# Normalising and the first tap moved to ScalarE, and an order of its own for the first turn of layer 1

## Chip, cores and metric

One core of one Trainium2 chip. The metric is the device time of one execution in microseconds; of three runs of the kernel before, the median was 862.69 us (862.49 to 867.14). Instructions run on five engines, each with a queue of its own that is worked through in order: TensorE (PE), VectorE (DVE), ScalarE (ACT), GpSimd (POOL) and SyncE (SP, which issues the DMAs). They meet at semaphores only.

## The reference

Two layers over x of shape (8, 256, 256), that is 2048 rows of 256. Each layer computes `x = x + attn(layernorm(x)) + ffn(layernorm(x))`.

Layer 0: softmax attention over 8 key heads with 4 query groups, plus a memory term, and a gated FFN of 2048 columns with 4-bit weights. Layer 1, which the change is about:

```python
xc = silu(causal_conv(xn, conv_w, taps=4) + conv_b)          # depthwise, along the sequence
q, k = l2n(xn @ Wq.T), l2n(xn @ Wk.T)                        # 16 heads of 16
v = ln(xn @ Wv.T) * vn_g + vn_b
i = sigmoid(xc @ ig_w.T + ig_b); gamma = sigmoid(xc @ gamma_w.T + gamma_b)
mem[t] = gamma[t] * mem[t-1] + i[t] * k[t] * v[t]            # scan along the sequence
o = ln(ln(mem) * q) * gn_g + gn_b
attn = (o * sigmoid(xc @ og_w.T + og_b)) @ Wo.T
ffn = (sigmoid(xn @ T1.T) * (xn @ T2.T)) @ T3.T              # T: weights rounded to -1, 0, 1; 704 columns
```

## The kernel before

Every factor of a matrix product is split into a high part (rounded to the format that TensorE reads) and a low part, the remainder, so that a product is three products (high by high, high by low, low by high). The high part is made by ScalarE, the low part by VectorE or GpSimd (`xn_low`, `hidden_low`, `next_low`, `output_low`).

**Layer 0** (`layer0`, to 610.7 us of the trace) is a pipeline over 64 units, one head of one batch element and one FFN pair each; `schedule()` puts extra steps at units. In units 58 to 65 it also prepares layer 1: SyncE loads the raw weights, ScalarE rounds them (`next_high`, two halves a unit, from unit 60), GpSimd subtracts (`next_low(n)`, one a unit, units 61 to 64). SyncE then loads three pieces of the FFN's signs into the buffers that these leave; piece 2 needs `next_low(3)`. ScalarE copies the three pieces (`next_signs`), and each copy waits until all three have landed. After each batch element's FFN VectorE adds it to X and takes mean and variance for layer 1's norm, and GpSimd makes `rstd` of the variance (step `"mlp"`); for the last element GpSimd does so at the start of layer 1.

**Layer 1** (`layer1`) treats the rows in 4 groups of 512 (two batch elements b = 0, 1; 4 row tiles t; 2 column blocks k or m). The first half of a group's work (projections, convolution, gates, FFN up) is "early", the second half (scan, norms, output, FFN down) is "late". `turns` runs five turns `turn(late, early, ahead)`: (None, 0, 1), (0, 1, 2), (1, 2, 3), (2, 3, None), (3, None, None). "Ahead" is the start of the group behind the early one: normalise, transposes, first projections, first taps. I call them turn 0 to 4; turn 0 has no late group. What an engine does in a turn is written out by hand as a sequence of calls (`if late is not None: ...`), and this sequence is its queue.

The steps that the change touches:
- `normalise(g)`: four instructions, one a row tile of 256, `(x - mean) * rstd` into `xn`, on VectorE (L1445); TensorE transposes `xn` (`xn_turn`, L1668), ScalarE evicts it twice (`xn_high`, L1266 and L1267: `xn_hi` and the padded `xpad`).
- `convolve(g, taps)`: tap 0 is a `tensor_scalar` per column block (`x*w0 + bias`, L1457), taps 1 to 3 are `scalar_tensor_tensor` (L1460), all on VectorE. Then `convolved`: two sigmoids on ScalarE (L1306), the products on GpSimd (L1216), high part on ScalarE (L1310), low part on GpSimd (L1219).
- `query_key(g, t)`, `value(b)`, `gamma(m)`, `gate(t)` and `ffn_up(c)` on TensorE (L1649, L1702). `projected` (L1277, L1278), `values_squared`, `sigmoid(c)` (L1293), `hidden_high(c)` (L1300), `decays`, `gate` on ScalarE evict them.
- `norms()` on VectorE: sums of squares (L1472), an inverse root by steps (L1422 to L1429), the scaled values (L1482). `hidden(c)` on VectorE (L1489) is the FFN's product; chunk c + 1 on TensorE waits for `hidden(c)`.
- `values(b)` (four steps, L1118), `through_input_gate(b)` (L1152) and the late group's `memory_scaled`, `gated` (L1118): one half on VectorE, the other on GpSimd.

In turn 0 TensorE's sequence was: transposes, queries/keys 0 and 1, FFN chunk 0, 1, queries/keys 2, values 0, 1, chunk 2, queries/keys 3, chunk 3, gamma 0, chunk 4, gates 0, 1, chunk 5, group 1's transposes 0, gamma 1, gates 2, 3, transposes 1, group 1's queries/keys 0, 1. Then turn 1 begins with `b_turn` (L1755), which needs both halves of `through_input_gate`, and FFN chunk 0, which needs both halves of group 1's `xn_low`.

## Time and profile before

| what | us |
|---|---|
| median of 3 runs (lowest, highest) | 862.69 (862.49, 867.14) |
| profiled execution, its own time | 865.88 |
| its span | 864.0 |
| mean granted clock of TensorE | 0.938 |
| VectorE `L1445` normalise, 8 of them from 640 us on | 8.9 |
| ScalarE idle in front of `L1293`, 640 to 864 us | 40.6 |
| GpSimd `L1118` rows<-rows,par, 24 of them | 34.2 |

The span is the profiled execution from its first to its last instruction; its own time is 1.9 us more. Busy time of an engine says how full it is, not whether it sets the end. For that one looks at the timeline, where each row has the idle time of its engine before it and, behind the arrow, what ended it: the engine that is never idle in a stretch, or the waits handed from engine to engine, set its length. A granted clock of 1.0 is TensorE's level of 2.4 GHz, 0.5 that of 1.2 GHz; a figure between them is a mean over a stretch.

### The profile page before, as it was taken

Reading aid. Unit: us, or ns where it says so; the run is one execution under the profiler, and the core shown is the slowest. Engines: PE = TensorE matmul, PEld = TensorE weight load, DVE = VectorE, ACT = ScalarE, POOL = GpSimd, SP = SyncE. Lnnn points to the kernel's source line nnn. Section 1 sums busy time; section 2 is a strip of 40 time slices with the busy share of each in tenths; the row PEclk is TensorE's granted clock in tenths of the full one; section 3 lists DMA queues with packets and bytes.
Section 4 is the critical chain, followed back from the end, with each engine's and each line's share of the span. In section 5 each row is a group of like instructions: output and inputs, shape, how many; then the busy total and the mean of one; then the engine's idle time right before and its main releaser. Section 6 shows DMA issues by size and latency. Waiting matters only on the chain. (4 is left out here: it accounts for less than half of the span.)

```text
span 864.0 us, 15139 instructions
## 1 busy us (share of the span) xinstructions
PE 750.2 (87%) x5602; PEld 645.5 (75%) x5602; DVE 653.9 (76%) x1123; ACT 454.8 (53%) x722; POOL 420.1 (49%) x353
## 2 busy tenths in 40 slices
PE   3368799999999999999999999999568897888773
PEld 2266688888888888888888888887456686777672
DVE  6989877887777677686777777673664899998965
ACT  4246645655655655664665565565544453454411
POOL 2344444354257575667344435346354283663821
PEclk9579999999999999999999999999788899999985
DMA  5011121111001011011000000301100000000000
GB/s 156 25 38 39 38 76 44 48 36 45 20 15 38 24 47 46 20 50 27 9 21 10 12 21 3 93 3 41 48 0 1 0 1 25 1 17 10 0 25 24
DMA packets 22108, 25.88 MB, mean 30 GB/s; under 512 B 4499, under 2 KB 17171, under 8 KB 22037
## 3 DMA queue, kind: packets, MB, share of 16 engines
q1 hardware_dynamic: 22036, 24.93, 10.5%
q8 instruction: 45, 0.74, 0.3%
q14 instruction: 27, 0.21, 0.1%
HBM read 14.83 MB, written 3.28 MB: 21 GB/s over the span
## 5 line engine op out<-in xcount | busy, mean ns | idle before, releaser
L647 DVE TENSOR_REDUCE neg_max<-s_pair 128x4 f32<-128x1024 f32 x127 | 155.1, 1221 | 75.3 <-PE s_pair L861 75.1
L469 ACT ACTIVATE probs<-t_pair 128x1024 f32<-128x1024 f32 x128 | 131.2, 1025 | 136.8 <-PE t_pair L886 136.5
L366 POOL TENSOR_TENSOR hid<-g,hid 128x512 f32<-128x512 f32 x64 | 82.2, 1285 | 179.2 <-DVE g L758 146.1
L360 POOL TENSOR_TENSOR hid_lo<-hid,hid_hi 128x512 fp32r<-128x512 f32 x64 | 86.0, 1344 | 86.8 <-ACT hid_hi L492 86.7
L861 PE MATMUL s_pair<-K,Q 96*128 96x256 f32 x508 | 85.0, 291 | 15.6 <-DVE neg_max L647 9.2
L861 PEld LDWEIGHTS s_pair<-K,Q 96*128 96x128 f32 x508 | 75.8, 194 | 24.2 <-issue 8.1
L886 PE MATMUL t_pair<-Q,K 104*128 104x512 f32 x256 | 85.9, 417 | 0.3 <-DMA Q<-max_parts 0.3
L928 PE MATMUL down<-hi,hid_hi 128*128 128x256 f32 x256 | 84.0, 328 | 1.9 <-POOL hid_lo L360 1.9
L901 PE MATMUL misc<-probs,V 128*32 128x256 f32 x1024 | 69.2, 388 | 3.4 <-DVE kc L603 2.6
L928 PE MATMUL down<-lo,hid_hi 128*128 128x256 f32 x256 | 71.9, 281 | 0.0
L928 PE MATMUL down<-hi,hid_lo 128*128 128x256 f32 x256 | 71.7, 280 | 0.0
L1118 POOL TENSOR_TENSOR rows<-rows,par 128x512 f32<-128x512 f32 x24 | 34.2, 1425 | 71.6 <-DVE rows L1524 54.0
L928 PEld LDWEIGHTS down<-hi,hid_hi 128*128 128x128 f32 x256 | 48.1, 188 | 27.9 <-issue 24.9
L1702 PE MATMUL lbank<-lo,hi 128*128 128x512 f32 x192 | 54.7, 431 | 12.6 <-DVE l_hid L1489 12.3
L789 PE MATMUL gate<-xn_hi,hi 128*128 128x256 f32 x256 | 57.0, 304 | 0.0
L1702 PEld LDWEIGHTS lbank<-lo,hi 128*128 128x128 f32 x192 | 37.9, 205 | 25.0 <-DVE l_hid L1489 16.6
L750 DVE SCALAR_TENSOR_TENSOR g<-g,gate 128x512 f32<-128x512 f32 x64 | 42.7, 668 | 18.0 <-ACT g L495 17.9
L503 ACT ACTIVATE g<-g 128x512 f32<-128x512 f32 x64 | 40.2, 628 | 29.9 <-DVE g L750 29.9
L1649 PE MATMUL lbank<-hi,lo 128*128 128x512 f32 (+1 forms) x192 | 53.3, 378 | 1.2 <-DVE lo L1129 1.2
L789 PE MATMUL up<-xn_hi,hi 128*128 128x256 f32 x256 | 52.2, 286 | 0.0
L789 PE MATMUL up<-xn_lo,hi 128*128 128x256 f32 x256 | 51.9, 285 | 0.0
L789 PE MATMUL up<-xn_hi,lo 128*128 128x256 f32 x256 | 51.9, 285 | 0.0
(254 smaller groups left out, 1979.5 us busy)
## 6 DMA issues: line engine op xcount, KB each, us to landing
stage<-in_ternary SPq DMA_DIRECT2D x18, 256.0 KB, 2.8
Q<-q_hi SPq DMA_DIRECT2D x64, 64.0 KB, 2.0
stage<-in_scales SPq DMA_DIRECT2D x8, 384.0 KB, 3.4
X<-in_x SPq DMA_DIRECT2D x8, 256.0 KB, 4.2
Q<-q_lo SPq DMA_DIRECT2D x32, 64.0 KB, 2.0
Q<-max_parts SPq DMA_DIRECT2D x128, 4.0 KB
out<-X SPq DMA_DIRECT2D x8, 256.0 KB, 2.1
signs<-w_stage SPq DMA_DIRECT2D x9, 128.0 KB, 1.8
```

The source lines that it names most:

```text
L360: pool.tensor_tensor(hid_lo[:, m % 2, :, :].rearrange("p a n -> p (a n)"), hid[:, m % 2, :], hid_hi[:, m % 2, :, :].rearrange("p a n -> p ...
L366: pool.tensor_tensor(hid[:, m % 2, :], g[:, m % 2, :], hid[:, m % 2, :], ALU.mult).then_inc(S["hid_done"], 1)
L469: act.activation(probs[:, u % 2, th, :], t_pair[:], ACT.Exp, scale=SCALE).then_inc(S["probs_done"], 1)
L647: dve.tensor_reduce(neg_max[:, u % 2, 4 * jp:4 * jp + 4], score_banks(u, jp)[:].rearrange("p (s n) -> p s n", n=SEQ), AX_X, ALU.max, negat ...
L750: dve.scalar_tensor_tensor(out=g[:, m % 2, :], in0=g[:, m % 2, :], scalar=1.0, in1=gate[:], op0=ALU.add, op1=ALU.mult).then_inc(S["u_done" ...
L789: mm = pe.matmul(out, lhs[a][k], rhs[b][k], start=(n == 0), stop=(n == 3 * KC - 1))
L861: mm = pe.matmul(score_banks(u, jp)[:, 512 * j + SEQ * s:512 * j + SEQ * s + SEQ], Q[0:KROWS, quad, 2 * jp + j, P * s:P * s + P], K[0:KROW ...
L886: mm = pe.matmul(t_pair[:, 512 * jp:512 * jp + 512].rearrange("p (j n) -> p j n", j=2), K[rows, quad, hq, P * th:P * th + P], Q[rows, quad ...
L901: mm = pe.matmul(misc[32 * j:32 * j + 32, 0:SEQ], V[:, th, h, :], probs[:, u % 2, th, SEQ * j:SEQ * j + SEQ], start=(th == 0), stop=(th == ...
L928: mm = pe.matmul(down[:, D * t:D * t + D], h[:, m % 2, n, P * t:P * t + P], w[:, a, n, 2 * D:3 * D], start=(a == 0 and t == 0 and n == 0 a ...
L1649: mm = pe.matmul(dst, lhs[a](k), rhs[b](k), start=(n == 0), stop=(last and n == 3 * KC - 1))
L1702: mm = pe.matmul(banks[bank][:], w[:, k, P * c:P * c + P], x[:, k, :], start=(n == 0), stop=(n == 3))
```

## The change

1. `normalise` moves from VectorE to ScalarE, in all turns: `Identity` with `scale=rstd` and `bias=shift`, both per row. `shift = -mean * rstd` is new: two GpSimd instructions of two columns behind each batch element's `rstd` in layer 0, and two at the start of layer 1. In turns 1 and 2 ScalarE does it between `convolved` and `output_squared(0)`.
2. Tap 0 moves to ScalarE as `first_tap` (semaphore `conv_first`), in turns 0, 1 and 2 ahead of the next group's `projected(0)`. `conv_step` counts 6 instead of 8.
3. `next_low` runs one unit earlier in layer 0.
4. Turn 0 gets sequences of its own on all engines. The other turns keep theirs, other than for 1 and 2. `norms` is cut in two (`norms_summed`, `norms`), one behind the other in the later turns; `convolved` on ScalarE likewise (`convolution_gated`).

```diff
-                    pool.tensor_tensor(rs, rs, half[:], ALU.pow)
+                    pool.tensor_tensor(rs, rs, half[:], ALU.pow).then_inc(S["pool_link"], 1)
+                    sh = keep["shift"][:, 2 * b:2 * b + 2]
+                    pool.wait_ge(S["pool_link"], linked())
+                    pool.tensor_tensor(sh, keep["mv"][:, 2 * b:2 * b + 2, 0], rs, ALU.mult).then_inc(S["pool_link"], 1)
+                    pool.wait_ge(S["pool_link"], linked())
+                    pool.tensor_scalar(sh, sh, -1.0, None, ALU.mult)
...
-                if 0 <= u - NEXT_AT - 3 < 4:
-                    next_low(u - NEXT_AT - 3)
+                if 0 <= u - NEXT_AT - 2 < 4:
+                    next_low(u - NEXT_AT - 2)
...
+                def normalise(g):                      # on ScalarE
+                    ...
+                    for t in range(TPG):
+                        one = slice(g * TPG + t, g * TPG + t + 1)
+                        x = flat(X[:, one, :]).rearrange("p (j k) -> p k j", k=KC)
+                        inc(act.activation(xn[:, t, :, :], x, ACT.Identity, scale=rstd[:, one], bias=shift[:, one]), "xn_ready")
+                def first_tap(g):
+                    ...
+                        inc(act.activation(dst, xpad[:, k, :, 0:SEQ], ACT.Identity, scale=conv[:, k, 0:1], bias=conv[:, k, TAPS:TAPS + 1]), "conv_first")
...
                 if late is None:                       # GpSimd, turn 0
                     xn_low(pool, early, 1)
                     scaled()
+                    convolved()
+                    output_weights()
+                    hidden_low(pool, early, 1)
+                    values(pool, early, 0)
+                    hidden_low(pool, early, 2)
+                    through_input_gate(pool, early, 0)
+                    hidden_low(pool, early, 3)
+                    through_input_gate(pool, early, 1)
+                    hidden_low(pool, early, 4)
+                    hidden_low(pool, early, 5)
+                    xn_low(pool, ahead, 1)
+                    return
...
                 if late is None:                       # ScalarE, turn 0
+                    normalise(early)
                     xn_high(early, 0)
                     xn_high(early, 1)
-                    constants()
+                    act.wait_ge(once["loaded"], 16 * N_LOADS)
+                    first_tap(early)
+                    gate_constants()
                     projected(early, 0)
                     projected(early, 1)
+                    values_squared(0)
+                    values_squared(1)
+                    projected(early, 2)
+                    projected(early, 3)
+                    convolution_gated()
+                    sigmoid(0)
+                    output_weights()
+                    convolved()
+                    hidden_high(0)
+                    hidden(1)
+                    gate(0)
+                    hidden(2)
+                    normalise(ahead)
+                    decays(0)
+                    gate(1)
+                    hidden(3)
+                    gate(2)
+                    gate(3)
+                    hidden(4)
+                    decays(1)
+                    hidden(5)
+                    xn_high(ahead, 0)
+                    xn_high(ahead, 1)
+                    queries_kept()
+                    hidden_high(5)
+                    first_tap(ahead)
+                    projected(ahead, 0)
+                    projected(ahead, 1)
+                    return
...
                 if late is None:                       # VectorE, turn 0
-                    normalise(early)
                     xn_low(dve, early, 0)
-                    convolve(early, range(0, 2))
+                    convolve(early, range(1, TAPS))
                     ...                                # the gates' bias
+                    norms_summed()
+                    hidden(0)
+                    norms()
+                    hidden(1)
+                    hidden_low(dve, early, 0)
+                    values(dve, early, 1)
+                    for c in range(2, FFN_CHUNKS):
+                        hidden(c)
+                    xn_low(dve, ahead, 0)
+                    convolve(ahead, range(1, 2))
+                    return
...
                     query_key(early, 1)                # TensorE, turn 0
+                    value(0)
+                    value(1)
+                    query_key(early, 2)
+                    query_key(early, 3)
+                    ffn_up(0)
+                    ffn_up(1)
+                    gate(0)
+                    ffn_up(2)
+                    gamma(0)
+                    gate(1)
+                    ffn_up(3)
+                    gate(2)
+                    gate(3)
+                    ffn_up(4)
+                    gamma(1)
+                    ffn_up(5)
+                    xn_turn(ahead, 0)
+                    xn_turn(ahead, 1)
+                    query_key(ahead, 0)
+                    query_key(ahead, 1)
+                    return
```

## Rows read from the trace of the kernel before

**Rows 1.** The page's engine table: busy us (share of the span) xinstructions.

```profile
PE 750.2 (87%) x5602; PEld 645.5 (75%) x5602; DVE 653.9 (76%) x1123; ACT 454.8 (53%) x722; POOL 420.1 (49%) x353
```

**Rows 2.** Busy by stretch: us; PE, PEld, DVE, ACT, POOL busy; granted clock; DMA, GB/s.

```profile
611.00:662.90 51.90, 40.33 (x168) 32.15 (x168) 31.20 (x47) 27.04 (x48) 23.79 (x26) 0.84 0.06 14
662.90:721.70 58.80, 48.46 (x249) 40.29 (x249) 52.25 (x87) 26.05 (x47) 33.19 (x25) 0.91 0.00 1
...
612.50:621.00 8.50, 7.30 (x21) 5.80 (x22) 6.21 (x9) 4.59 (x9) 5.13 (x6) 0.51 0.30 81
...
643.00:649.00 6.00, 5.83 (x16) 4.62 (x17) 5.04 (x7) 1.36 (x3) 5.76 (x6) 0.57 0.00 0
...
729.00:734.00 5.00, 5.00 (x18) 4.03 (x17) 4.76 (x12) 1.10 (x3) 1.77 (x2) 0.66 0.00 0
```

**Rows 3.** Timeline, end of layer 0, GpSimd, ScalarE, VectorE: start, us, what [idle before].

```profile
595.32 1.85 POOL L354 TENSOR_TENSOR lo<-queries,hi 128x768 fp32r<-128x768 f32 x1
...
601.43 1.84 POOL L354 TENSOR_TENSOR lo<-w_stage,hi 128x768 fp32r<-128x768 f32 x1
603.23 1.72 POOL L360 TENSOR_TENSOR hid_lo<-hid,hid_hi 128x512 fp32r<-128x512 f32 x1
610.92 0.53 POOL L1190 MEMSET rows<- 128x512 f32 x1 [5.98 <-POOLq L109]
...
606.42 2.86 ACT L482 ACTIVATE hi<-stage 128x1536 fp32r<-128x1536 bf16 x2 [4.05 <-DMA w_stage<-signs]
...
608.19 0.25 DVE L629 BATCH_NORM_AGGREGATE l_mv<-stats 128x2 f32<-128x6 f32 x2
```

**Rows 4.** Timeline of GpSimd, a batch's end in layer 0.

```profile
566.85 0.20 POOL L347 TENSOR_SCALAR l_rstd<-l_mv 128x2 f32<-128x2 f32 x1
...
569.33 1.29 POOL L360 TENSOR_TENSOR hid_lo<-hid,hid_hi 128x512 fp32r<-128x512 f32 x1 [1.51 <-ACT hid_hi L492]
```

**Rows 5.** Timeline, layer 1, turns 0 and 1: TensorE and GpSimd.

```profile
624.86 2.11 PE L1702 MATMUL lbank<-lo,hi 128*128 128x512 f32 x8 [1.97 <-DVE l_hid L1489]
...
643.17 2.05 PE L1649 MATMUL lbank<-lo,hi 128*128 128x512 f32 x4 [6.61 <-POOL lo L1219]
...
666.74 3.75 PE L1702 MATMUL lbank<-lo,hi 128*128 128x512 f32 x8 [0.22 <-POOL lo L1129]
...
664.09 1.25 POOL L1152 TENSOR_TENSOR rows<-qk,gates 128x512 f32<-128x512 f32 x1
```

**Rows 6.** Timeline of ScalarE around the start of layer 1.

```profile
599.88 0.38 ACT L513 ACTIVATE o_sb<-misc 128x256 f32<-128x256 f32 x1
...
616.25 0.71 ACT L1251 ACTIVATE o_hi<-rows,const 128x512 fp32r<-128x512 f32 x1
616.86 0.61 ACT L1252 ACTIVATE lo<-rows 128x512 fp32r<-128x512 f32 x1
```

**Rows 7.** Timeline of VectorE, layer 1.

```profile
624.72 1.38 DVE L1445 TENSOR_SCALAR rows<-X,l_mv,l_rstd 128x256 f32<-128x256 f32 x4
...
634.31 3.41 DVE L1472 TENSOR_REDUCE ss<-sq 128x96 f32<-128x1536 f32 x2
...
643.54 0.68 DVE L1489 TENSOR_TENSOR l_hid<-sig,lbank 128x512 f32<-128x512 f32 x1
...
672.84 0.69 DVE L1513 TENSOR_REDUCE sm<-osq 128x32 f32<-128x512 f32 x1 [2.40 <-ACT osq L1343]
...
678.41 4.46 DVE L1445 TENSOR_SCALAR rows<-X,l_mv,l_rstd 128x256 f32<-128x256 f32 x4
...
713.97 2.86 DVE L1457 TENSOR_SCALAR shared<-xpad,conv 128x512 f32<-128x512 f32 x2
...
740.94 0.68 DVE L1489 TENSOR_TENSOR l_hid<-sig,lbank 128x512 f32<-128x512 f32 x1
```

**Rows 8.** Timeline, end of turn 1: GpSimd's gating, VectorE's low parts.

```profile
710.73 3.06 POOL L1118 TENSOR_TENSOR rows<-rows,par 128x512 f32<-128x512 f32 x2 [2.96 <-DVE rows L1558]
...
716.75 1.28 DVE L1563 TENSOR_TENSOR o_lo<-lbank,o_hi 128x512 fp32r<-128x512 f32 x2
```

More of the change, by code:

```diff
@@ L1199, in _ @@
             pool.tensor_tensor(rstd[:, last], rstd[:, last], half[:], ALU.pow).then_inc(once["rstd_done"], 1)
+            pool.wait_ge(once["rstd_done"], 2)
+            pool.tensor_tensor(shift[:, last], mv[:, last, 0], rstd[:, last], ALU.mult).then_inc(once["rstd_done"], 1)
+            pool.wait_ge(once["rstd_done"], 3)
+            pool.tensor_scalar(shift[:, last], shift[:, last], -1.0, None, ALU.mult).then_inc(once["rstd_done"], 1)
             def scaled():
@@ L1233, in turn @@
                     through_input_gate(pool, early, 0)
-                if late is not None:
-                    gated(pool, late, 0)
+                gated(pool, late, 0)
                 if early is not None:
@@ L1374, in turn @@
                     hidden(3)
+                    convolution_gated()
                     convolved()
-                if late is not None:
-                    output_squared(0)
+                if ahead is not None:
+                    normalise(ahead)
+                output_squared(0)
                 if early is not None:
@@ L1381, in turn @@
                     sigmoid(4)
-                if late is not None:
-                    output_squared(1)
+                output_squared(1)
                 if early is not None:
@@ L1398, in turn @@
                     hidden_high(5)
-                if late is not None:
-                    for b in halves:
-                        output_high(b)
+                for b in halves:
+                    output_high(b)
                 if ahead is not None:
+                    first_tap(ahead)
                     projected(ahead, 0)
@@ L1683, in value @@
                     wait("xpad_done", b + 1)
+                    wait(f"xn_lo_done{b}", 1)
                     wait("decay_done", 0)
@@ L1804, in turn @@
                     ffn_up(3)
-                if late is not None:
-                    ffn_down(0)
-                    ffn_down(1)
+                ffn_down(0)
+                ffn_down(1)
                 if early is not None:
@@ L1823, in turn @@
                     query_key(ahead, 1)
-                if late is not None:
-                    for b in halves:
-                        o_turn(b)
-                    for b in halves:
-                        output(b)
+                for b in halves:
+                    o_turn(b)
+                for b in halves:
+                    output(b)
             turns(turn)
```

128 lines of the change are left out of this document (57 added, 71 removed).

## The prediction

> **What bounds the kernel now.** I read the engine table first [rows 1]: TensorE is busy 87% of the span, VectorE 76%, ScalarE 53%, GpSimd 49%. That average mixes two stages, so I went on to the stretches [rows 2]. Layer 0 ends at 610.7; layer 1 is five turns from 611 to 864. In turn 0 (611 to 662.9) VectorE works 31.2 of 51.9 us and TensorE 40.3: neither is full, so waits set it. In turn 1 (662.9 to 721.7) VectorE works 52.25 of 58.8: there VectorE is the bound, and turn 2 is alike. The timeline of turn 1 confirms it: VectorE has two gaps, of 2.4 us each, near the start (the second in [rows 7]), and hardly any from 673.7 on. The last two turns issue what they did before, so I take them as unchanged.
>
> In what follows all times are on the trace's own clock; "new" times of turn 0 leave the earlier start of layer 1 out and it is added at the end.
>
> **Part A, the weight splits one unit earlier.** GpSimd's last `next_low` runs at 601.43 for 1.84 us, ahead of the last `hidden_low`, which runs from 603.23 to 604.95; the last down product waits for that, and VectorE's last aggregate, behind the product, ends at 608.44 [rows 3]. SyncE issues the third load of signs only when that `next_low` is done, at 603.3; it lands 3.1 us later. ScalarE waits 4.05 us for it, starts the three sign copies at 606.42 and ends them at about 610.7 (1.43 each). Layer 1's first GpSimd instruction is at 610.92. One unit earlier the fourth `next_low` stands at 595.32, where the third is now, done at 597.17; the load is issued then and lands some 3.1 us later, 600.3. ScalarE copies from 602.3 on, three times 1.43: done at 606.6. `hidden_low` starts when its input is there, 602.4, ends about 603.7, the product starts 1.25 us earlier, VectorE ends at 608.44 - 1.25 = 607.2. That is now the later one: layer 1 starts at about 607.5, 3.4 us earlier. Least: 1.5 (a copy is late for another reason); most: 3.6, ScalarE's path. The first `next_low` has to wait for a copy that ScalarE makes earlier in its queue than anything GpSimd needs next, and falls into an idle time like that before `hidden_low` at 569.33: nothing.
> GpSimd's two new tiny operations (the shift) follow each batch's power, seven times: 0.2 us each and a gap (the scale at 566.85 took 0.20). Behind them GpSimd idles 1.51 us before `hidden_low` at 569.33 [rows 4]: hidden; if not, 0.6 us times 7.
>
> **Part B, turn 0.** Today the chain runs through GpSimd: TensorE waits 6.61 us at 643.17 for the low part of the convolution, since ScalarE comes to the convolution's sigmoids only behind four FFN chunks; at the turn's end the second input gate runs from 664.09 to 665.34 on GpSimd and TensorE's transposes and chunk 0 of turn 1 (666.74) come after it [rows 5]. The new order, step by step:
> Normalise on ScalarE. The trace has no 256-wide instruction there with two pointer operands. A plain one takes 0.38 us (599.88); of two 512-wide ones the one with a pointer scale takes 0.71 (616.25), the other 0.61 (616.86) [rows 6]: 0.38 + 0.1 + 0.1 = 0.58, less 0.1 of overlap as between those two, about 0.48 each, 1.9 for four against VectorE's 1.38 [rows 7]. Bounds 0.3 and 0.7 each. TensorE's eight transposes, at half clock, take about as long and cover it: the first two tiles are ready at 612.65 instead of 612.4, and the evictions start at 613.7, as before. The first tap is 0.61 + 0.2 - 0.1 = 0.7 each, 616.05 to 617.5, and the first projection is ready only at 618.6; VectorE's taps 1 to 3, six of them, end by 622.3 at 0.9 each, and nobody asks for them before 628.9. The Trainium skill, "ScalarE: Activation LUTs", on the ACTIVATE instruction, gives 186 ns + 0.833 ns an element and 93 ns more for each pointer operand. By it four rows are 2.0 us and two taps 1.4; the trace agrees on the pointer operand (0.10 us in rows 6), and the rule speaks against moving them only where ScalarE is late.
> TensorE: queries/keys 0 and 1 end at 620.9, as now, at a granted clock of 0.51, the 1.2 GHz level [rows 2]. From there a 512-wide pass is 0.23 us (eight in 2.11 with the tail [rows 5]): values 2.9 (24 passes of half the width), to 623.8; queries/keys 2 and 3, 1.4 each, to 626.6; FFN chunk 0 (1.85) to 628.4. ScalarE squares the last projection by 627.7, loads its table (1.28) to 628.9, does the convolution's two sigmoids (1.1) to 630.0 and chunk 0's to 630.6. VectorE's two square sums end at 629.5, `hidden(0)` at 631.2, the norms at 637.0 (today the sums take 3.41 from 634.31 on and the norms end at 643.54, so 5.8 [rows 7]), `hidden(1)` at 637.7. GpSimd meanwhile has the convolution's four operations (5.3 us today, at 1.3 each), from 629.6 to 634.8. So TensorE idles from 628.4 to 631.3, does chunk 1, waits to 634.8, does gate 0 and starts chunk 2 at 637.8, behind the norms. Here I expect the clock to be halved for some us, as it was after the idle time before 643 (0.57) [rows 2]; up to 637.8 that costs nothing, since the norms end last.
> From 637.8: chunk 2, gamma 0, gate 1 (1.85 + 1.4 + 1.6) to 642.7; chunk 3 waits for `hidden(2)`, behind `values(1)` on VectorE (2.8 beside an idle GpSimd, 4.0 beside a busy one), 643.1; chunk 3, gates 2 and 3, chunk 4, gamma 1 to 651.4; chunk 5 to 653.3; transposes to 654.0. Then ScalarE's evictions to 655.0, VectorE's low part to 655.8, queries/keys of group 1 to 658.6, the two input transposes to 659.6. ScalarE: queries kept by 657.1, `hidden_high(5)` 657.7, GpSimd `hidden_low(5)` 659.0 and `xn_low` 660.3. So chunk 0 of turn 1 starts at 660.3 where it was 666.74 [rows 5]; the scans, behind one tap on VectorE, end at 662.4 where they ended at 667.8.
> At 666.74 the clock was low, chunk 0 took 3.75 where eight passes take 2.11 at full clock, the centring as much longer, and VectorE waited 2.40 us at 672.84 [rows 5, 7]; at turn 2's start neither was so. I expect turn 2's picture: centring from 662.2 to 664.1, squares to 664.7, VectorE's sums from 665.1 to 666.4 where they end at 674.43 (the second 0.9 behind the row of 672.84): 8.0 us earlier. Were the clock low there, 5.3; were it full throughout and layer 1 begun warm, 10.5.
>
> **Part C, normalise and first tap in turns 1 and 2.** The four normalising instructions take VectorE 4.46 us in turn 1 and 4.45 in turn 2, but 1.38 in turn 0: in the former GpSimd works beside them. The two first taps take 2.86 beside GpSimd [rows 7], and 1.0 without it. Both leave VectorE. How much of it arrives? In turn 2: the norm ends at 731.99; `hidden(1)` has its sigmoid at 731.9 and runs at once; the scaling, low part and centring take 4.0, to 736.6. Then `hidden(2)` needs chunk 2, and TensorE, at a clock of 0.66 from 729 to 734 [rows 2], comes to it only at 736.4: product to 738.3, sigmoid to 738.9, `hidden(2)` at 738.9 against 740.94 [rows 7]. So 2.0 of the 4.45 arrive; at full clock 3.6 would; 0.5 if TensorE or the sigmoid slips as much again. ScalarE's own 1.9 us go in ahead of `output_squared(0)` at 748.32, behind which it idles 2.6 us: nothing. The same holds for turn 1.
> Of the first tap 0.25 arrives: with it gone VectorE is ready at 714.0, but it then needs `o_hi`, which hangs on GpSimd's gating (from 710.73, 3.06 and 1.3 us, to 715.14), TensorE's transposes and an eviction, together to 716.5; its two low parts begin at 716.75 today [rows 8]. ScalarE does the taps after `o_hi`, 716.9 to 718.4, just before VectorE wants them at 717.7. Bounds: 0 and, GpSimd being freed of contention, 1.0. Together 2.25 a turn, 4.5 for two.
>
> **Sum.** 3.4 + 8.0 + 4.5 = 15.9 us. The profiled execution took 865.88 for a span of 864.0; it becomes 850.0. The median of the runs shown, 862.69, is 3.2 lower; from it 846.8, which I predict.
>
> **Rivals.**
> One, the clock stays up: TensorE, with fewer gaps, is at full clock when layer 1 starts (the pause before it shrinks from 5.9 to about 4 us) and at the middle of turns 1 and 2. Then B is 10.5 and C 2 x 3.9: 841. For it: turn 0 ran at full clock from 621 to 636 with a pause of 2.0 in it. Against: at 729 to 734 it was 0.66 behind a pause of 2.7 which stays. Chance 0.18.
> One more on that side: VectorE stays the bound to the end of turns 1 and 2, and all of what it is relieved of arrives, 4.45 + 2.86 a turn, 14.6 for two: 3.4 + 8.0 + 14.6 = 26.0, 836.7. For it: 52.25 busy of 58.8 [rows 2]. Against: TensorE comes to chunk 2 only at 736.4, and `o_hi` only at 716.5. Chance 0.03. The Trainium skill, "GPSIMD Engine Reference", section Specifications, says that the SBUF interfaces are shared with VectorE, with contention for instructions in a two-port mode or with two SBUF inputs. The 4.46 against 1.38 us [rows 7] agree, and by it VectorE's other instructions with two SBUF inputs would keep their own contention.
> Two, less arrives: VectorE's gain in turns 1 and 2 is met by TensorE at half clock (0.5 each), and turn 0's handover stays at the low clock (5.3): 3.4 + 5.3 + 1.0 = 9.7, 853. Chance 0.2.
> Three, layer 0's end doesn't move, as another wait holds the copies, and two holds as well: 856.4; with turn 0's chain longer by 3 us, 859. Chance 0.06 for all of the near-nothing cases (over 858.4).
> Four, slower: the norms stand between `hidden(0)` and `hidden(1)` on VectorE, so TensorE has gaps from 628.4 to 637.8 and could stay at 1.2 GHz for the rest of turn 0. What lies behind 637.8 is 18.4 us of passes (four chunks at 1.85, two gammas, three gates, transposes, two queries/keys); doubled, chunk 0 of turn 1 starts at 680 instead of 666.74, 13.5 later, and with A and C off it is +5.6: 868. It decides from about 14 us of extra passes on. Against: after the pause of 6.6 the clock, 0.57 from 643 to 649 [rows 2], was full again after that. Chance 0.03.
>
> **Chances and range.** The forecast (844 to 850.5 as its own range) has 0.50. A measurement of this kernel tells 0.5%, 4.3 us, from no change. Faster 0.91, same 0.06, slower 0.03. The range leaves out the 836.7, the first rival's far end, and cases three and four: 839 to 854.
>
> **What would show it.** A: the gap before ScalarE's sign copies gone, GpSimd's first memset of layer 1 at 607.5. B: TensorE's longest wait in turn 0 under 3 us, chunk 2 behind the norms, turn 1's scans ending at 659 on the new clock. C: no wait for `hidden(1)`, one of about 1 us or less before `hidden(2)`, one of 2.5 us before the low parts of o. Wrong would be: more than 3 us of waiting ahead of `hidden(2)`, a projection late behind ScalarE's normalise, or turn 0 longer than 49 us.

## The result, and the profile after

The changed kernel takes 850.32 us (median of 4 runs, 848.63 to 851.37), the kernel before, run beside it, 863.62 (862.49 to 867.14). The medians are 13.3 us apart. The ratio over all executions, which is not exactly that of the medians, is 0.9833, with a 95% interval of 0.9806 to 0.9861: 14.4 us faster (12.0 to 16.8). All gains below are worked out from such ratios, each against executions of the kernel before that ran beside it. The profiled execution took 849.49 us for a span of 847.5, 16.5 less than the 864.0 of before, at a mean granted clock of 0.949 (0.938).

The engine table of the page, to be read beside [rows 1]: VectorE gives up 20 us of busy time, ScalarE takes on 14. TensorE is busy 8 us less for the same number of matmuls, since fewer of them ran at the lower clock.

```profile
PE 742.0 (88%) x5602; PEld 638.1 (75%) x5602; DVE 633.5 (75%) x1099; ACT 468.4 (55%) x746; POOL 423.2 (50%) x369
```

The stretches that answer to [rows 2]. The first three lines are turns 0, 1 and 2, here cut at VectorE's first sums of the memory's centred squares (`sm<-osq`) in turns 1 to 3 ([rows 2] cuts earlier, where the scans start, so its lines and these don't compare one to one); the other lines are where the granted clock fell, or didn't.

```profile
607.60:663.60 56.00, 44.17 (x196) 35.03 (x196) 30.84 (x43) 36.70 (x65) 27.86 (x30) 0.88 0.05 13
663.60:716.00 52.40, 46.20 (x248) 39.27 (x248) 45.49 (x81) 27.87 (x50) 29.40 (x22) 0.93 0.03 11
716.00:765.80 49.80, 43.44 (x248) 36.73 (x248) 45.30 (x81) 28.32 (x51) 29.88 (x22) 1.00 0.03 11
...
628.00:636.00 8.00, 5.72 (x17) 4.03 (x18) 7.69 (x14) 3.40 (x7) 4.98 (x4) 0.80 0.00 0
...
664.00:672.00 8.00, 6.44 (x28) 5.47 (x29) 6.82 (x18) 2.36 (x5) 2.79 (x3) 0.79 0.00 0
705.00:711.00 6.00, 5.04 (x28) 4.83 (x28) 4.61 (x6) 3.83 (x7) 2.26 (x2) 0.72 0.13 44
717.00:723.00 6.00, 5.00 (x29) 4.43 (x30) 5.66 (x16) 2.38 (x5) 1.42 (x2) 1.00 0.00 0
```

Those sums make good milestones: every kernel has them and little overlaps across them. The distances from one to the next, read from the profiled execution of every kernel of this study (us; "start" is GpSimd's first memset of layer 1, and all kernels but the first two are described below):

| kernel | span | start | turn 0 | turn 1 | turn 2 | turn 3 | rest |
|---|---|---|---|---|---|---|---|
| before | 864.0 | 610.92 | 61.92 | 53.88 | 54.55 | 51.48 | 31.25 |
| after | 847.5 | 607.63 | 56.01 | 52.43 | 49.77 | 50.86 | 30.80 |
| e1_split_early | 858.6 | 608.35 | 60.28 | 55.10 | 54.87 | 49.26 | 30.74 |
| e2_moves | 858.4 | 611.23 | 62.54 | 51.66 | 51.34 | 50.84 | 30.79 |
| e3_order_only | 857.4 | 610.65 | 54.70 | 54.84 | 54.51 | 51.46 | 31.24 |
| e4_norm_alone | 858.2 | 611.54 | 61.90 | 52.03 | 52.65 | 49.31 | 30.77 |
| e5_norm_only | 857.7 | 610.94 | 62.01 | 52.02 | 52.65 | 49.31 | 30.77 |
| e6_tap_only | 864.3 | 610.13 | 63.21 | 53.50 | 54.76 | 51.49 | 31.21 |
| e7_fill | 844.3 | 607.43 | 56.35 | 50.23 | 50.37 | 48.86 | 31.06 |
| e8_high_first | 845.5 | 605.82 | 54.89 | 51.36 | 51.38 | 51.01 | 31.04 |
| e9_no_moves | 845.9 | 605.78 | 54.59 | 52.04 | 51.73 | 50.96 | 30.80 |
| e10_twice | 847.0 | 606.02 | 56.47 | 51.36 | 51.38 | 50.93 | 30.84 |
| e11_both | 840.6 | 606.98 | 55.30 | 49.22 | 49.22 | 48.88 | 31.00 |
| e12_both_no_moves | 847.1 | 606.92 | 55.61 | 50.88 | 52.97 | 49.45 | 31.27 |

So the 16.5 us of the span came from: start 3.29, turn 0 5.91, turn 1 1.45, turn 2 4.78, turns 3 and 4 1.07. The table also shows how far to trust one execution: e1 runs the same layer 1 as before, and its single turns differ by 0.3 to 2.2 us, with a TensorE that was at the lower clock in other places. What a part is worth is therefore taken from the ratios, and the profile is used for where it happens.

**The end of layer 0**, GpSimd and then ScalarE, beside [rows 3]. The fourth `next_low` is gone from between 601.43 and 603.23; `hidden_low` starts when its input is there, the sign copies follow without a wait.

```profile
595.17 1.86 POOL L359 TENSOR_TENSOR lo<-w_stage,hi 128x768 fp32r<-128x768 f32 x1
...
600.03 1.29 POOL L371 TENSOR_TENSOR hid<-g,hid 128x512 f32<-128x512 f32 x1 [1.75 <-DVE g L763]
602.28 1.27 POOL L365 TENSOR_TENSOR hid_lo<-hid,hid_hi 128x512 fp32r<-128x512 f32 x1 [0.96 <-ACT hid_hi L497]
607.63 0.52 POOL L1195 MEMSET rows<- 128x512 f32 x1 [4.08 <-POOLq L109]
...
602.11 2.85 ACT L487 ACTIVATE hi<-stage 128x1536 fp32r<-128x1536 bf16 x2
604.86 1.47 ACT L487 ACTIVATE hi<-w_stage 128x1536 fp32r<-128x1536 bf16 x1
608.24 2.14 ACT L1288 ACTIVATE rows<-X,l_shift,l_rstd 128x256 f32<-128x256 f32 x4 [1.92 <-POOL half L1197]
```

**The middle of turn 0**, VectorE and TensorE, beside [rows 5, 7]: `hidden(0)`, the norms (their first and last instruction), `hidden(1)`; then FFN chunks 1 and 2. The wait of 6.61 us for the convolution's low part is gone; in its place stand 3.03 and 1.82, both for VectorE. The clock was low behind the first: chunk 1 takes 3.42, chunk 2 2.14.

```profile
627.58 0.69 DVE L1556 TENSOR_TENSOR l_hid<-sig,lbank 128x512 f32<-128x512 f32 x1 [1.19 <-ACT sig L1335]
628.18 1.16 DVE L1541 SCALAR_TENSOR_TENSOR ss<-ss,eps 128x192 f32<-128x192 f32 x1
...
634.82 0.68 DVE L1556 TENSOR_TENSOR l_hid<-sig,lbank 128x512 f32<-128x512 f32 x1
...
628.32 3.42 PE L1765 MATMUL lbank<-lo,hi 128*128 128x512 f32 x8 [3.03 <-DVE l_hid L1556]
...
635.55 2.14 PE L1765 MATMUL lbank<-lo,hi 128*128 128x512 f32 x8 [1.82 <-DVE l_hid L1556]
```

**The handover to turn 1**: ScalarE, VectorE, GpSimd, TensorE. ScalarE has its queue without a gap from 651.6 on; its first taps come last before VectorE's tap 1, which waits 2.70 us for them and then runs beside GpSimd's `xn_low`.

```profile
653.50 1.09 ACT L1370 ACTIVATE q_kept<-qk 128x1024 f32<-128x1024 f32 x1
654.45 0.29 ACT L1371 ACTIVATE rq<-ss 128x64 f32<-128x64 f32 x1
654.59 0.66 ACT L1342 ACTIVATE hi<-l_hid 128x512 fp32r<-128x512 f32 x1
655.11 1.54 ACT L1296 ACTIVATE shared<-xpad,conv 128x512 f32<-128x512 f32 x2
...
656.10 2.66 DVE L1525 SCALAR_TENSOR_TENSOR shared<-xpad,conv,shared 128x512 f32<-128x512 f32 x2 [2.70 <-ACT shared L1296]
658.68 2.41 DVE L1572 TENSOR_TENSOR_SCAN rows<-shared,lbank 128x256 f32<-128x256 f32 x4
661.01 2.71 DVE L1525 SCALAR_TENSOR_TENSOR shared<-xpad,conv,shared 128x512 f32<-128x512 f32 x4
663.64 1.27 DVE L1580 TENSOR_REDUCE sm<-osq 128x32 f32<-128x512 f32 x2
...
655.33 1.29 POOL L1140 TENSOR_TENSOR lo<-l_hid,hi 128x512 fp32r<-128x512 f32 x1 [3.83 <-ACT hi L1342]
656.58 1.63 POOL L1134 TENSOR_TENSOR lo<-xpad,lo 128x512 fp32r<-128x512 f32 x1
...
658.47 2.06 PE L1765 MATMUL lbank<-lo,hi 128*128 128x512 f32 x8 [1.08 <-POOL lo L1134]
660.36 1.95 PE L1826 MATMUL lbank<-const,rows 128*128 128x128 f32 x16
```

**Turns 1 and 2**, VectorE and TensorE, beside [rows 7, 8]: `hidden(1)`, `hidden(2)`, the first sum of squares, the low parts of o. Chunk 1 on TensorE waits for `hidden(0)`, 3.25 us in turn 1 and 2.41 in turn 2; behind the longer wait the clock was low (3.55 against 2.12 us).

```profile
669.78 0.69 DVE L1556 TENSOR_TENSOR l_hid<-sig,lbank 128x512 f32<-128x512 f32 x1 [0.80 <-ACT sig L1335]
...
675.87 0.69 DVE L1556 TENSOR_TENSOR l_hid<-sig,lbank 128x512 f32<-128x512 f32 x1 [0.88 <-ACT sig L1335]
676.48 3.40 DVE L1536 TENSOR_REDUCE ss<-sq 128x96 f32<-128x1536 f32 x2
...
705.03 1.29 DVE L1630 TENSOR_TENSOR o_lo<-lbank,o_hi 128x512 fp32r<-128x512 f32 x2 [2.46 <-ACT o_hi L1398]
...
721.34 0.68 DVE L1556 TENSOR_TENSOR l_hid<-sig,lbank 128x512 f32<-128x512 f32 x1
...
726.85 0.69 DVE L1556 TENSOR_TENSOR l_hid<-sig,lbank 128x512 f32<-128x512 f32 x1 [0.42 <-ACT sig L1335]
...
665.56 3.55 PE L1765 MATMUL lbank<-lo,hi 128*128 128x512 f32 x8 [3.25 <-DVE l_hid L1556]
...
718.00 2.12 PE L1765 MATMUL lbank<-lo,hi 128*128 128x512 f32 x8 [2.41 <-DVE l_hid L1556]
```

### The profile page after: what moved, and what is told of

It reads as the page before. It is cut to its first block and busy times, and to the rows that moved or that the text cites. A ratio compares the mean times of both kernels' runs of the same rounds, so it can differ in the third digit from the quotient of the medians.

```text
span 847.5 us, 15157 instructions
## 1 busy us (share of the span) xinstructions
PE 742.0 (88%) x5602; PEld 638.1 (75%) x5602; DVE 633.5 (75%) x1099; ACT 468.4 (55%) x746; POOL 423.2 (50%) x369
## 5 line engine op out<-in xcount | busy, mean ns | idle before, releaser
L1711 PE MATMUL lbank<-hi,lo 128*128 128x512 f32 (+1 forms) x192 | 51.0, 367 | 2.8 <-ACT lo L1308 1.6
```

The lines of the kernel that those rows point to most:

```text
L1711: mm = pe.matmul(dst, lhs[a](k), rhs[b](k), start=(n == 0), stop=(last and n == 3 * KC - 1))
```

## Experiments: the parts one by one

**e1_split_early: part A alone.**

```diff
-                if 0 <= u - NEXT_AT - 3 < 4:
-                    next_low(u - NEXT_AT - 3)
+                if 0 <= u - NEXT_AT - 2 < 4:
+                    next_low(u - NEXT_AT - 2)
```

> The kernel before with part A alone: next_low one unit earlier. Theory: layer 1's first GpSimd instruction moves from 610.9 to 607.6 and nothing else changes, so 3.3 us off (859.4 from 862.7), with all of layer 1 shifted as a block. Rival: the copies of the signs are not what layer 0's end waits for in the end, or the shorter pause changes TensorE's clock at the start of layer 1: then under 1 us or over 5 us.

861.93 us against 864.94, ratio 0.9978 (0.996 to 0.9995): 1.9 us, with an interval of 0.4 to 3.5; the medians are 3.0 apart. Within one execution the distance from GpSimd's last `hid<-g` to its first memset of layer 1 is cleaner, as it leaves out how long the rest of layer 0 took: 10.73 us before (600.19 to 610.92), 7.60 in the changed kernel, 7.32 here. Part A is worth 3.1 to 3.4 us at its place, and the ratio allows that only at the end of its interval. The two figures differ by the moves: from the last `hidden_low` to that memset it is 5.35 or 5.36 us in the five kernels that have both part A and the moves to ScalarE (after, e7, e8, e10, e11), and 5.07 in the three that have part A without the moves (e1, e9, e12).

**e3_order_only: turn 0's order alone**, with normalise and tap 0 on VectorE and `next_low` where it was. Against the changed kernel:

```diff
                 if late is None:                       # VectorE, turn 0
+                    normalise(early)
                     xn_low(dve, early, 0)
-                    convolve(early, range(1, TAPS))
+                    convolve(early, range(0, TAPS))
...
                     for c in range(2, FFN_CHUNKS):
                         hidden(c)
+                        if c == 2:
+                            normalise(ahead)
                     xn_low(dve, ahead, 0)
-                    convolve(ahead, range(1, 2))
+                    convolve(ahead, range(0, 2))
```

> The kernel before with turn 0's new sequences on all engines, but normalise and tap 0 still on VectorE (the next group's normalise behind hidden(2)) and the old place of next_low. Theory: the reordering by itself takes about 6 us off (5 in turn 0, the rest as TensorE starts turn 1 at full clock): 856 to 857.5. Rival: the order only pays because ScalarE took work off VectorE in turn 0, and here VectorE ends the turn late: under 2 us off.

859.52 us, ratio 0.9937 (0.9912 to 0.9963): 5.4 us. In the profile turn 0 is 7.2 us shorter, more than in the changed kernel (5.9), and turns 1 to 4 are within 1.0 us of before.

**e2_moves: normalise and tap 0 on ScalarE, in the old order of turn 0.** It has points 1 and 2 of the change, and none of 3 and 4.

> The kernel before with normalise and tap 0 on ScalarE, the old order in turn 0 and the old place of next_low. Theory: 2.0 to 3.4 us in each of turns 1 and 2 ahead of the sums of squares, 0.25 behind, nothing in turn 0: 4.5 to 7 us off, 856 to 858. Rival one: all that VectorE is relieved of arrives, 14 us off. Rival two: the moves pay only with the new turn 0, so under 1.5 us off here.

860.37 us, ratio 0.994 (0.9919 to 0.9962): 5.2 us. Turns 1 and 2 are 2.2 and 3.2 shorter, turn 0 is 0.6 longer. The three parts alone add up to 1.9 + 5.4 + 5.2 = 12.5 us of the 14.4, the same within their intervals (by the medians 3.0 + 5.4 + 4.6 = 13.0 of 13.3).

**e5_norm_only and e6_tap_only: the two moves apart.** e5 has `normalise` and `shift` of the change in the kernel before, e6 has `first_tap`.

> The kernel before with the normalisation alone moved to ScalarE (old order of turn 0, first taps stay on VectorE). Theory: normalise carries nearly all of the gain of turns 1 and 2 (together 5.4 us for both moves): turns 1 and 2 shorter by 2 to 3 us each, turn 0 level, since there VectorE doesn't bind, 860.0 us. Rival: the taps carry part, since with them off VectorE its low parts of o come earlier by more than 0.25 us: 861.5 us.

> The kernel before with the first tap alone moved to ScalarE. Theory: 0.25 us a turn at most, since VectorE's low parts of o then wait for o_hi instead (a wait of 2.4 to 2.6 us before them), and in turn 0 ScalarE comes to the taps no earlier than VectorE did, up to 0.6 us lost there: level with before within 0.1%, 864 against 864 us. Rival: the 2.86 us of two taps beside GpSimd arrive in turns 1 and 2: 3 to 5 us faster.

e5: 857.04 us, ratio 0.9919 (0.9888 to 0.9949), 7.0 us; by the profile turns 1 and 2 are 1.9 shorter each. e6: 865.44 us, ratio 1.0007 (0.9986 to 1.0028); turn 0 is 1.3 longer, turns 1 and 2 together 0.2 shorter. What the moves gained in the kernel before came from normalising, as far as the times can tell; part of the 7.0 may be turn 3, 2.2 shorter in e5's profile, though the change leaves that turn alone.

**e4_norm_alone: the same four instructions on VectorE, only earlier.** In the kernel before, VectorE's normalise stood behind `memory_normed`, where GpSimd is busy; here it stands ahead of it, where GpSimd is idle. Nothing leaves VectorE.

```diff
+                if ahead is not None:
+                    normalise(ahead)
                 if late is not None:
                     memory_normed()
-                if ahead is not None:
-                    normalise(ahead)
```

> The kernel before with one change: VectorE's normalise of the next group stands ahead of memory_normed, where GpSimd is idle, and not behind it, where GpSimd works. If contention with GpSimd makes the four instructions 4.46 us, they take about 1.4 here in turns 1 and 2, hidden(2) comes 2 us earlier in each and the kernel is 3 to 5 us faster (858 to 860). If their length belongs to them, they stay at 4.4 and the time stays within 1 us or gets longer.

859.94 us, ratio 0.994 (0.9917 to 0.9963): 5.2 us, as much as e2. VectorE in turn 1 (compare 4.46 in [rows 7]):

```profile
675.53 1.38 DVE L1445 TENSOR_SCALAR rows<-X,l_mv,l_rstd 128x256 f32<-128x256 f32 x4
...
686.11 0.69 DVE L1489 TENSOR_TENSOR l_hid<-sig,lbank 128x512 f32<-128x512 f32 x1 [0.74 <-ACT sig L1293]
686.72 3.41 DVE L1472 TENSOR_REDUCE ss<-sq 128x96 f32<-128x1536 f32 x2
```

Four instructions that cost 4.46 us beside GpSimd cost 1.38 without it. In turn 1 the sum of squares starts 13.28 us behind the first of `sm<-osq` here, the same 13.28 in e5 and 15.13 before: 1.85 arrive whether 3.1 us of VectorE's time go or all 4.46. The rest goes mostly to waits that then appear, for chunk 2's sigmoid (0.74 here, 1.02 in e5) and in e5 for chunk 1's too (0.75), and to instructions that now run beside GpSimd (in e5 `hidden_low(0)` takes 1.26 us, here 0.72).

**e9_no_moves: the changed kernel with both moves taken back** and e4's place for normalise. If moving work to ScalarE is what matters, this one loses it.

> Turn 0's new order and the early next_low, but normalise and tap 0 stay on VectorE, with normalise ahead of memory_normed in turns 1 and 2, where GpSimd is idle. Theory (contention, not the engine, made normalise dear; the three parts add up): layer 1 takes within 2 us of what it takes in the changed kernel, 848 to 852. Rival (the moves to ScalarE are worth their 5 to 7 us on top): 854 to 857.

850.23 us, ratio 0.9831 (0.9802 to 0.986): level with the changed kernel. Layer 1 took 240.12 us of the span, there 239.87. The balance has two sides: turn 0 is 1.4 us shorter than in the changed kernel, and turns 1 and 2 together are 1.0 longer than in e8 and e10, which have the moves. VectorE at the handover, to be read beside the changed kernel's:

```profile
651.85 1.00 DVE L1504 TENSOR_SCALAR shared<-xpad,conv 128x512 f32<-128x512 f32 x2 [0.29 <-ACT xpad L1282]
652.77 1.41 DVE L1507 SCALAR_TENSOR_TENSOR shared<-xpad,conv,shared 128x512 f32<-128x512 f32 x2
655.13 2.42 DVE L1555 TENSOR_TENSOR_SCAN rows<-shared,lbank 128x256 f32<-128x256 f32 x4 [0.95 <-PE lbank L1820]
657.47 2.71 DVE L1507 SCALAR_TENSOR_TENSOR shared<-xpad,conv,shared 128x512 f32<-128x512 f32 x4
660.37 0.69 DVE L1563 TENSOR_REDUCE sm<-osq 128x32 f32<-128x512 f32 x1 [0.18 <-ACT osq L1361]
```

VectorE did tap 0 in 1.0 us at 651.85, in time that it otherwise idles, tap 1 in 1.41 ahead of GpSimd's `xn_low`, and now waits for TensorE before the scans. With tap 0 on ScalarE, turn 0 is 56.01, 56.35 and 56.47 us (after, e7, e10), without it 54.70 and 54.59 (e3, e9): the move costs 1.6 us there. This is the price in this order of ScalarE's queue, not of the move as such. Where `hidden_high(5)` goes first (e8, e11 and e12, below), turn 0 is 54.89 and 55.30 with the move and 55.61 without it: VectorE's tap 1 then runs beside GpSimd's `hidden_low(5)` as well as its `xn_low`, and takes 3.38 us in e12.

```profile
654.27 3.38 DVE L1507 SCALAR_TENSOR_TENSOR shared<-xpad,conv,shared 128x512 f32<-128x512 f32 x2
```

**e10_twice: is ScalarE's work free in turns 1 and 2?** The changed kernel, writing the four normalised tiles twice in each of these turns.

```diff
                 if ahead is not None:
-                    normalise(ahead)
+                    normalise(ahead, True)             # the four instructions two times
```

> The changed kernel; in turns 1 and 2 ScalarE writes the four normalised tiles twice, 2.1 us more of its time in each. Theory: ScalarE has slack there and nothing gets longer, within 0.5 us a turn. Rival: ScalarE is so near the chain that the 2 us come back, at least in part, through hidden_high(3) and the evictions behind it: 1 to 2 us a turn.

848.69 us, ratio 0.9813 (0.979 to 0.9836). The second set (2.15 us at 684.41) is there in the trace. Turns 1 and 2 are 51.36 and 51.38 us, together 0.5 more than in the changed kernel (52.43 and 49.77) and the same as in e8 (51.36 and 51.38), which writes them once: no loss. ScalarE's side of the move is free, with at least 2.1 us of room.

## Experiments: what holds the changed kernel, and a faster one

**e7_fill.** In turns 1 to 3 TensorE waits for `hidden(0)` ahead of FFN chunk 1, and VectorE is then late for `hidden(2)`. Here queries/keys 2 and value 0, which need nothing of VectorE, go ahead of chunk 1, and ScalarE's evictions follow.

```diff
                     ffn_up(0)                          # TensorE
-                    ffn_up(1)
                     query_key(early, 2)
                     value(0)
+                    ffn_up(1)
...
-                    hidden_high(0)                     # ScalarE
-                    hidden(1)
                     projected(early, 2)
                     values_squared(0)
+                    hidden_high(0)
+                    hidden(1)
                     values_squared(1)
```

> The changed kernel; in turns 1 to 3 TensorE does queries/keys 2 and values 0 ahead of FFN chunk 1 (in the pause of 2.4 to 3.3 us in which it waits for hidden(0)), and ScalarE evicts them before hidden_high(0). If it is TensorE's pause and the low clock behind it that hold hidden(2) back, chunk 1 runs in about 2.1 us instead of 3.55 in turn 1, VectorE no longer waits for hidden(1) and hidden(2), and the sums of squares come 2.5 to 3 us earlier in turn 1, 0.4 in turn 2, 2 in turn 3: 3 to 6 us less than the changed kernel. If VectorE was the bound there all along, under 1 us.

843.69 us, ratio 0.9758 (0.9725 to 0.9791), against the changed kernel's 0.9833. TensorE in turn 1; VectorE has no wait before `hidden(1)` and `hidden(2)`:

```profile
665.69 2.11 PE L1765 MATMUL lbank<-lo,hi 128*128 128x512 f32 x8 [0.43 <-DVE l_hid L1556]
...
674.02 0.68 DVE L1556 TENSOR_TENSOR l_hid<-sig,lbank 128x512 f32<-128x512 f32 x1
674.62 3.40 DVE L1536 TENSOR_REDUCE ss<-sq 128x96 f32<-128x1536 f32 x2
```

The wait is 0.43 instead of 3.25 us, chunk 1 runs at full clock (2.11 us instead of 3.55), and turns 1 to 3 are 2.2, -0.6 and 2.0 shorter. Turn 2 had been at full clock in the changed kernel's profile; here the clock was low at its end (0.86 from 755 to 766), which costs 1.1 us. From the sums to the first sum of squares it is 10.84 us in both turns, against 12.84 and 11.39 in the changed kernel and 12.97 to 12.99 in e8 and e10.

That distance, and the two behind it, tell the parts apart better than whole turns. From the sums to the sum of squares, in turns 1 and 2: 15.13 and 14.82 before, 13.28 and 12.87 in e4, 13.28 and 12.88 in e5. From the sum of squares to the low parts of o: 28.77 to 28.82 in the seven kernels with the first tap on VectorE (before, e1, e3, e4, e5, e9, e12), 28.54 to 28.58 in the seven with it on ScalarE. From there to the next sums: 9.82 to 9.97 or 10.85 to 11.04, whatever the kernel, but for turn 2 of e12 (below). In the changed kernel that last distance is 11.04 in turn 1, at a clock of 0.84 from 705 to 716, where the output's pairs of 256-wide matmuls take 0.63 us each, and 9.83 in turn 2, at 1.00, where they take 0.40.

**e8_high_first.** In turn 0 ScalarE does the high half of hidden 5 and the first taps ahead of the kept queries, for which nobody waits so soon.

```diff
-                    queries_kept()
                     hidden_high(5)
                     first_tap(ahead)
+                    queries_kept()
```

> The changed kernel; at the end of turn 0 ScalarE does hidden_high(5), the next group's first tap and only then keeps the queries (before: queries kept, hidden_high(5), first tap). My prediction had turn 0 1.8 us too short. If the late first tap on ScalarE and VectorE's second tap running beside GpSimd's xn_low made that (2.66 us for two, behind a wait of 2.70), the scans of turn 1 start 1 to 1.7 us earlier and FFN chunk 0 of turn 1 about 1 us: 1 to 1.5 us less than the changed kernel. Rival: queries/keys of group 1 end last anyway, under 0.4.

848.7 us, ratio 0.982 (0.9792 to 0.9848). Turn 0 is 1.1 shorter, 54.89: VectorE's wait for the first tap is 1.61 instead of 2.70, and chunk 0 of turn 1 starts without one.

```profile
653.15 2.67 DVE L1525 SCALAR_TENSOR_TENSOR shared<-xpad,conv,shared 128x512 f32<-128x512 f32 x2 [1.61 <-ACT shared L1296]
```

The direction is that of the theory, but by the times the gain isn't shown: it is smaller than the interval of the comparison.

**e11_both and e12_both_no_moves.** e11 is the changed kernel with both edits. e12 has them too, but with both moves taken back as in e9. They tell what the moves are worth once TensorE doesn't hold VectorE up.

> The changed kernel with both improvements found so far: chunk 1 of the FFN behind queries/keys 2 and value 0 on TensorE in turns 1 to 3 (843.7 us alone), and in turn 0 ScalarE's high half of hidden 5 and the first taps ahead of the kept queries (turn 0 shorter by 1.1 us). Theory: the two lie in different turns and add up: turn 0 about 55, turns 1 and 2 about 50 each, 842.6 us. Rival: what turn 0 gives up is lost at the handover to turn 1, where TensorE then waits for something else (chunk 0 of turn 1 already started without a wait in the kernel with the high half first): 843.7, no better than the reordering of TensorE alone.

> As the last kernel, but normalise and first tap are VectorE's own, as before the change, with the normalisation ahead of the memory's norms, where GpSimd idles. Theory (in turns 1 and 2 the moves to ScalarE are worth what taking the normalisation off GpSimd's busy time is worth, while TensorE holds VectorE up anyway): with TensorE's holdup reduced VectorE is the bound again, so the moved 1.4 us of normalising and some 1 to 1.5 us of taps now count in turns 1 and 2, about 1.5 us a turn: 845.5 us. Rival: as much stays hidden as in the kernel without the moves and with TensorE's old order (level with the changed kernel): 842.6.

e11: 843.29 us, ratio 0.9761 (0.9736 to 0.9787), no better than e7 by its time, so that the gain of e8 does not show here either; its span, 840.6, is the shortest of all profiled, but that is one execution. e12: 848.77 us, ratio 0.9818 (0.9793 to 0.9844), by the medians 5.5 us more than e11 on the same chip, by the ratios 4.9. So there the moves do pay, which they didn't in e9. Of e12, VectorE's normalising in turn 1, the residual at the end of turn 2, and the stretch from 711.6 to 761.0, which is turn 2 (713.4 to 766.4) but for its last 5.4 us; e11 spent its turn 2 at a clock of 1.00:

```profile
664.31 1.37 DVE L1492 TENSOR_SCALAR rows<-X,l_mv,l_rstd 128x256 f32<-128x256 f32 x4
...
760.61 0.69 DVE L1619 TENSOR_TENSOR X<-lbank,X 128x512 f32<-128x512 f32 x1 [1.87 <-PE lbank L1713]
...
711.60:761.00 49.40, 42.62 (x229) 36.44 (x228) 45.99 (x81) 24.17 (x43) 30.21 (x22) 0.93 0.02 6
```

In turn 1 the low parts of o start 39.40 us behind the first of the sums in e11 (662.28 to 701.68) and 40.93 in e12 (662.53 to 703.46): 1.53 us, of which the four instructions are 1.3, from 664.31 to 665.61, and the taps, which replace a wait of 2.45, the rest. That is the 1.5 us a turn that was expected. Turn 2 lost 3.75 us: again these 1.5, and 2.2 behind the low parts of o (12.03 against 9.83), where TensorE, now at times at the lower clock, kept VectorE waiting (1.87). Whether the extra work on VectorE causes the lower clock or only met it in this execution is open.

## Why the prediction came out right, step by step

The forecast was 846.8 us, within 839 to 854; it came out 3.5 above the forecast. In the profile the sum was 15.9 us, and 16.5 came. The forecast subtracted it from a median that lay 3.2 us below its profiled execution, while after the change the median lies 0.8 above its own; so the profiled executions are 16.4 us apart where the medians are 13.3 apart, and the median before was 0.9 higher in the comparison (863.62) than at the forecast. That 15.9 and 16.5 agree is partly luck: by the table B was 2.1 too large, C 1.7 too small, and 1.1 us came in the last two turns, which I had taken as unchanged. In turn 3 the same code takes 51.5 us in three of the profiles and 49.3 in three others, so that these 1.1 us need no cause in the change. The prediction had set B's end at the end of the sums (674.43 before, 664.91 now); by that mark B is 6.2, 1.8 less than predicted, and C 5.9.

**A, 3.4 predicted, 3.1 to 3.4 measured.** The sign copies start 602.11 (602.3 predicted), the first memset is at 607.63 (607.5). The reasoning that the product behind `hidden_low` becomes the later of the two held. Rival three is out. The shift was taken as hidden. At the start of layer 1 the kernels with the moves are 0.28 us later (5.35 against 5.07, above); whether by the shift's instructions was not tested.

**B, 8.0 predicted, 5.9 measured.** The order was sized well: e3, without the moves, brought 7.2 us. Up to the norms the steps came within 1.1 us: chunk 2 at 635.55, predicted 637.8 less the 3.3 of the earlier start, 634.5. Most of this is the norms' first instruction, 1.16 us where it took 0.36 before; GpSimd's products run until 629.12 beside it. The clock was low about where it was predicted (0.80 from 628 to 636) and full afterwards, 1.00 from 636 to 662: rival four is out, and so is the half-clock handover of rival two. The term that was mis-sized is the handover: of the 2.1 us that B lacks, 1.4 are the difference to e9 (56.01 against 54.59), which has the same order without the moves. I wrote "the scans, behind one tap on VectorE, end at 662.4" (659.1 on the new clock) and had priced TensorE's centring as what comes last. They ended at 661.1, and the sums, which no wait precedes (663.64), follow VectorE. ScalarE's queue is the reason: the two evictions of `xn`, the kept queries, `hidden_high(5)` and the first taps add up to 4.9 us without a gap (651.59 to 656.53), so tap 1 only starts at 656.10. In e9, where VectorE does both taps itself, it is done with them at 654.2, on this kernel's clock (layer 1 starts 1.85 later) at 656.0. And tap 1 then ran into GpSimd's `xn_low`: 2.66 us instead of 1.41. I had followed the first tap as work that must be ready and not as the last item of a full queue. Four normalising rows took 2.14 us and two taps 1.54 where the prediction had 1.9 and 1.4, so the price was nearly right, and it is the place in the queue that costs. The estimates from the Trainium skill, "ScalarE: Activation LUTs", section "What ACT_TABLE_LOAD costs", were 2.0 and 1.4 us, a little under what was measured.

**C, 4.5 predicted; 1.45 and 4.78, together 6.2, in the profile, 5.2 (3.3 to 7.0) by e2's time.** The split into what leaves VectorE and what arrives held. Of 4.46 us 1.85 arrive in turn 1 (e5, predicted 2.0), and part of what is missing is where it was put: `hidden(2)` waits for chunk 2's sigmoid, 0.88 in turn 1 and 0.42 in turn 2. Another part is not: `hidden(1)` in turn 1, for which no wait was predicted, waits 0.80. In turn 2 chunk 1 ran at full clock, and from the sums to the sum of squares it took 11.39 us instead of 14.82: 3.4, near the 3.6 that the prediction names for full clock. That is rival one's condition, met in one turn of two. Turn 1 gained 2.3 up to the sum of squares and 0.2 by the taps, and lost 1.1 at its end, where the clock was low (11.04 against 9.97); turn 2 gained 3.4 and 0.3, and another 1.1 at its end, where the clock was low before the change and not after (9.83 against 10.92). So the two turns differ by where the clock was low, and the 1.1 cancel in the sum. Without them and with chunk 1 at least partly at the low clock in both turns, as in e8 and e10 (12.97 us to the sum of squares), C would be 2.2 + 1.8 + 0.5 = 4.5, an estimate from single executions: the prediction's figure, which had assumed the low clock in both. The first taps brought 0.2 to 0.3 a turn between the sum of squares and the low parts of o in every kernel (predicted 0.25), and the wait before the low parts of o is 2.46 and 2.45 (predicted about 2.5). ScalarE's side costs nothing (e10). The rival by which all of VectorE's relief arrives is out in the changed kernel; e12 against e11 shows what it takes for the 1.3 us of normalising to arrive in full: TensorE's chunk 1 and 2 in time.

**Its signs of being wrong.** TensorE's longest wait in turn 0 was to be under 3 us and is 3.03; the scans were to end at 659 and end at 661.1. Turn 0 was not to be longer than 49 us, with no mark named: to TensorE's first input transposes of turn 1 (656.35) it is 48.7, to VectorE's scans (658.68) 51.1. By the second mark this sign says wrong, and what it points at is the handover.

**What I had not seen** is that the moves weren't needed to reach this time. Most of the 4.46 us went with GpSimd's work beside it, and a swap of two calls on VectorE (e4) brings what the moves do (e2); in the changed kernel (e9) it leaves about 1 us of turns 1 and 2 and regains it in turn 0. The prediction had both figures, 4.46 and 1.38, and used them for the size alone. The Trainium skill, "GPSIMD Engine Reference", section Specifications, says that SBUF's interfaces are shared with VectorE, with contention for instructions in a two-port mode or with two SBUF inputs; The taps at the handover (1.41 in e9, 2.66 in the changed kernel), which read two inputs from SBUF, agree with the second kind. e4's rows (4.46 to 1.38) would be the first kind; no row here tells in which mode they ran.

## What to carry to other kernels

- An operation that takes three times as long in one place as in another, in the same shape, is first of all in the wrong place. Swap it with a neighbour before another engine is given the work: here the swap brought as much (5.2 us each in e4 and e2), and nothing on the other queue. Once VectorE is the bound again, giving the work away pays on top (e11 against e12).
- Relief of the busiest engine arrives only as far as its next wait; work out when that wait's input is there. Here it was 1.85 of 4.46 us, until TensorE had other work ahead of the chunk that waited, which made the gap short, kept the clock up at that chunk and gave another 6 us (ratio 0.9758 against 0.9833).
- Work moved to an engine with spare time must be priced by its place in that queue. In the middle of a turn ScalarE did it for nothing, even twice; at the handover, as the last of five items, it cost 1.6 us; with `hidden_high(5)` ahead, it cost nothing in the profiles.

## What the runs showed of the hardware that was not expected

- Two `scalar_tensor_tensor` of 128x512 take 1.41 us on VectorE, and 2.66 when GpSimd's `xn_low` runs beside them, which itself takes 1.63 us then; beside the scans, in e9, it took 1.18. With two GpSimd operations beside them, in e12, they took 3.38.
- TensorE's clock and single waits: behind each of the waits of 3.03 to 3.25 us for `hidden(0)` the chunk ran at least in part at the lower clock (3.02 to 3.69 us), and behind those of 1.98 and less for VectorE, with full clock ahead of them, it didn't (2.1 us). Between them the length alone doesn't decide: behind 2.39 a chunk took 2.12 us in e1 and 2.55 in the kernel before, behind 2.72 it took 2.12 in e6 and 3.60 in e4, and behind 2.00 it took 2.11 in e1 and 2.76 in e9.
- Executions of the same instructions differ in where the clock falls. e1's turn 3 is 2.2 us shorter than that of before with the same code in layer 1, and layer 0 up to GpSimd's last `hid<-g` varied by 2.8 us (601.03 in e1, 598.23 in e8). A single profile can't size an effect of 1 us here; a distance within one execution between two nearby instructions can.
